# Fifteen rounds of two bits in place of thirty of one: the threshold search of a router on one Trainium2 core

## What is computed

```python
N, k = 4096, 1024                      # tokens; places of one expert
scores = jax.nn.softmax(xt @ Wr, axis=-1)      # (N, 8)
G, idx = jax.lax.top_k(scores.T, k)            # per expert: the k best tokens
X_in = xt[idx]
...
out = zeros.at[idx.reshape(-1)].add(contrib)
```

## Time and profile before

| | us |
|---|---|
| runs timed | 1288.48, 1290.49, 1291.82; median 1290.49 |
| profiled execution, span | 1295.1 |
| first count of the search to the copy of the threshold, in it | 637.92 to 684.86 |

### The profile page before, as it was taken

The page is one execution under the profiler, slowest core; times in us unless marked ns, Lnnn a source line. Parts: engine busy times, 40 slices in busy tenths (PEclk is TensorE's granted clock), DMA queues, the critical chain, the costliest instruction groups (busy, mean ns, idle before and its releaser), DMA issues. The chain is left out here.

```text
span 1295.1 us, 25137 instructions
## 1 busy us (share of the span) xinstructions
PE 975.8 (75%) x8604; PEld 662.5 (51%) x8604; DVE 805.3 (62%) x1683; ACT 639.2 (49%) x2132; POOL 430.4 (33%) x332
## 2 busy tenths in 40 slices
PE   6779998989899999985613769747348787867665
PEld 3456565656656565664503556534225454545454
DVE  5777758687777767564657514112136878559995
ACT  3565767767676767671101323112038777643322
POOL 2334333333342423321000857886611312200221
PEclk9789899999999998987555789888759999868967
DMA  6564343434443434431402123445310000000000
GB/s 198 150 182 107 92 123 88 119 96 113 102 113 100 113 83 107 104 91 42 102 0 62 45 59 69 61 73 129 31 66 1 1 2 1 1 1 9 17 17 25
DMA packets 89009, 93.62 MB, mean 72 GB/s; under 512 B 18800, under 2 KB 62304, under 8 KB 88944
## 3 DMA queue, kind: packets, MB, share of 16 engines
q1 hardware_dynamic: 78576, 84.12, 24.7%
q0 software_dynamic: 10368, 8.66, 4.7%
HBM read 24.36 MB, written 10.70 MB: 27 GB/s over the span
## 5 line engine op out<-in xcount | busy, mean ns | idle before, releaser
L835 POOL TENSOR_TENSOR qk_cos<-qk_raw,const 128x512 f32<-128x512 f32 x128 | 183.2, 1432 | 313.0 <-ACT qk_raw L589 313.0
L575 ACT ACTIVATE prob<-psS,neg_max 128x96 f32<-128x96 f32 x512 | 167.9, 342 | 86.5 <-DVE neg_max L670 85.7
L442 PE MATMUL psQ<-a_xnT,weights 128*128 128x512 f32 x250 | 146.0, 668 | 2.1 <-ACT a_xnT L621 1.4
L550 PEld LDWEIGHTS psO<-probT,v_windows 96*64 96x64 f32 x2048 | 73.7, 143 | 142.6 <-ACT probT L649 121.1
L550 PE MATMUL psO<-probT,v_windows 96*64 96x64 f32 x2048 | 91.8, 235 | 43.9 <-ACT probT L649 43.9
L685 DVE TENSOR_TENSOR qk_roped<-qk_cos,qk_swapped 128x512 f32<-128x512 f32 x128 | 119.0, 929 | 5.9 <-DVE qk_swapped L676 5.5
L1508 POOL DMA_INDIRECT sums<-ex_y,ex_index x64 | 97.6, 1525 | 39.5 <-issue 23.5
L1497 POOL DMA_INDIRECT ex_rows<-rows,ex_index x64 | 67.1, 1048 | 121.8 <-DMA ex_index<-lists 102.6
L575 ACT ACTIVATION_READ_ACCUMULATOR prob<-psS,neg_max 128x1 f32 x512 | 105.4, 206 | 0.0
L1442 ACT ACTIVATE ex_hidden<-ex_psH,ex_b 128x512 f32<-128x512 f32 x64 | 43.7, 687 | 114.4 <-PE ex_psH L1401 59.7
L649 ACT COPY probT<-psT 96x512 f32<-96x512 f32 x128 | 76.8, 600 | 46.5 <-PE psT L530 46.5
(11 more groups left out here) (317 smaller groups left out, 1936.2 us busy)
## 6 DMA issues: line engine op xcount, KB each, us to landing
qk_swapped<-qk_raw SPq DMA_DIRECT2D x512, 64.0 KB, 2.0
v_windows<-v_tok SPq DMA_DIRECT2D x32, 384.0 KB, 4.4
v_windows<-v_tok SPq DMA_DIRECT2D x32, 256.0 KB, 3.6
mod<-mod_rows SPq DMA_DIRECT2D x12, 512.0 KB, 6.0
ex_w<-in_L_ffn_W SPq DMA_DIRECT2D x16, 256.0 KB
v_windows<-v_tok SPq DMA_DIRECT2D x32, 96.0 KB, 2.1
rows<-rt_h SPq DMA_DIRECT2D x8, 256.0 KB, 2.4
sums<-rt_zeros SPq DMA_DIRECT2D x8, 256.0 KB, 2.7
```

Source lines behind the costliest of these rows:

```text
L442: last = nc.tensor.matmul(bank, k.wqkvT[:, col:col + P], xnT[:, :], start=True, stop=True)
L550: ins = nc.tensor.matmul(psO[D * j:D * j + D, i * P + a * HALF:i * P + (a + 1) * HALF], vw[:, par, a, t, hd], probT[:, 2 * j + i, a * HALF ...
L575: last = nc.scalar.activation(prob[:, s, 2 * j + i, :], psS[:, s, j, i * KW:(i + 1) * KW], ACT.Exp, bias=nmax[:, s, 2 * j + i:2 * j + i + ...
L835: nc.gpsimd.tensor_tensor(rcos[:, half, :], raw[:, half, :], k.const[:, K_COS:K_COS + T], ALU.mult).then_inc(cos_done, 1)
```

## The change

Each round settles two bits. There are three candidates a round, the settled bits with 1, 2 and 3 in the two present bits. VectorE counts three times, into three columns of `reached`; one matmul adds three columns. `met` compares the three totals with 1024 and sums how many candidates hold (0 to 3) into `passed`; `step` is that number times the weight of the lower present bit, as an integer; one operation ORs it with the settled bits and, in four columns, with 0 to 3 in the next two bits. Column 0 of `cand` is what is settled, and two buffers of `cand` take turns. The fifteen rounds are written out on both engines, so that all addresses and wait values are constants. The table of constants gets 4 x 16 columns in place of 31.

```diff
-LOOK = 5
+ROUNDS = BITS // 2
...
-K_END = K_BITS + BITS + 1
+K_END = K_BITS + 4 * (ROUNDS + 1)
...
-    t[:, K_BITS:K_BITS + BITS] = 2.0 ** np.arange(BITS - 1, -1, -1)
+    for r in range(ROUNDS):
+        t[:, K_BITS + 4 * r:K_BITS + 4 * r + 4] = np.arange(4) * 4.0 ** (ROUNDS - 1 - r)
...
-        sT, hitT = sb("rt_scoresT", [P, 2 * P]), sb("rt_hitT", [P, 2 * P], BF16)
-        same, bits = sb("rt_same", [P, P], BF16), sb("rt_bits", [P, BITS + 1], I32)
-        cand, drop, reached = sb("rt_cand", [P, 1], I32), sb("rt_drop", [P, 1], I32), sb("rt_reached", [P, 1], BF16)
+        sT, hitT = sb("rt_scoresT", [P, 2 * P]), sb("rt_hitT", [P, 3, 2 * P], BF16)
+        same, bits = sb("rt_same", [P, P], BF16), sb("rt_bits", [P, 4 * (ROUNDS + 1)], I32)
+        cand, met, passed, step = sb("rt_cand", [P, 2, 4], I32), sb("rt_met", [P, 3]), sb("rt_passed", [P, 1]), sb("rt_step", [P, 1], I32)
+        reached = sb("rt_reached", [P, 3], BF16)
...
-            with pe.Fori(0, BITS // LOOK) as turn:
-                for i in range(LOOK):
-                    pe.wait_ge(counted, turn * LOOK + i + 1)
-                    nc.tensor.matmul(psC[:, 0:1], same[:, :], reached[:, :], start=True, stop=True).then_inc(totals, 1)
+            for n in range(ROUNDS):
+                pe.wait_ge(counted, 3 * n + 3)
+                nc.tensor.matmul(psC[:, 0:3], same[:, :], reached[:, :], start=True, stop=True).then_inc(totals, 1)
...
-            own.mark(nc.vector.tensor_copy(cand[:, :], k.const[:, K_BITS:K_BITS + 1]))
+            own.mark(nc.vector.tensor_copy(cand[:, 0, :], k.const[:, K_BITS:K_BITS + 4]))
...
-            def look(turn, i):
-
-                n = turn * LOOK + i
+            def look(n):
+
+                now, then = cand[:, n % 2, :], cand[:, 1 - n % 2, :]
                 with nc.allow_low_precision("counts up to 256 are exact"):
-                    nc.vector.tensor_scalar(hitT[:, :], sT[:, :], cand[:, :].bitcast(F32), 0.0, ALU.is_ge, ALU.add,
-                                            accum_out=reached[:, :]).then_inc(counted, 1)
+                    for c in range(3):
+                        nc.vector.tensor_scalar(hitT[:, c, :], sT[:, :], now[:, c + 1:c + 2].bitcast(F32), 0.0, ALU.is_ge, ALU.add,
+                                                accum_out=reached[:, c:c + 1]).then_inc(counted, 1)
                 dve.wait_ge(totals, n + 1)
-                at = lambda table, n: table[:, bass.ds(n, 1)]
                 dve.wait_ge(search.sem, search.mark(nc.vector.tensor_scalar(
-                    drop[:, :], psC[:, 0:1], float(CAP), at(k.const, n + K_BITS), ALU.is_lt, ALU.mult)))
+                    met[:, :], psC[:, 0:3], float(CAP), 0.0, ALU.is_ge, ALU.add, accum_out=passed[:, :])))
+                dve.wait_ge(search.sem, search.mark(nc.vector.tensor_tensor(
+                    step[:, :], passed[:, :], k.const[:, K_BITS + 4 * n + 1:K_BITS + 4 * n + 2], ALU.mult)))
                 dve.wait_ge(search.sem, search.mark(nc.vector.scalar_tensor_tensor(
-                    out=cand[:, :], in0=drop[:, :], scalar=at(bits, n + 1), in1=cand[:, :],
-                    op0=ALU.bitwise_xor, op1=ALU.bitwise_xor)))
-
-            with dve.Fori(0, BITS // LOOK) as turn:
-                search.turn(turn)
-                for i in range(LOOK):
-                    look(turn, i)
-                assert search.n == search.per
+                    out=then, in0=bits[:, 4 * n + 4:4 * n + 8], scalar=step[:, :], in1=now[:, 0:1].to_broadcast([P, 4]),
+                    op0=ALU.bitwise_or, op1=ALU.bitwise_or)))
+
+            search.turn(0)
+            for n in range(ROUNDS):
+                look(n)
```

More of the change, by code:

```diff
@@ L962, in phase_router @@
         pe_turned, thr_ready = sem("rt_pe_turned"), sem("rt_thr_ready")
-        search = Tally(sem("rt_search"), 2 * LOOK)
+        search = Tally(sem("rt_search"))
         block = ctx.enter_context(nc.Block())
@@ L1119, in look @@
                 dve.wait_ge(search.sem, search.mark(nc.vector.scalar_tensor_tensor(
-                    out=cand[:, :], in0=drop[:, :], scalar=at(bits, n + 1), in1=cand[:, :],
-                    op0=ALU.bitwise_xor, op1=ALU.bitwise_xor)))
-            with dve.Fori(0, BITS // LOOK) as turn:
-                search.turn(turn)
-                for i in range(LOOK):
-                    look(turn, i)
-                assert search.n == search.per
-            nc.vector.tensor_copy(wide_thr[:, :], cand[0:E0, :].bitcast(F32).to_broadcast([E0, P])).then_inc(thr_ready, 1)
+                    out=then, in0=bits[:, 4 * n + 4:4 * n + 8], scalar=step[:, :], in1=now[:, 0:1].to_broadcast([P, 4]),
@@ L1130, in _ @@
+                    op0=ALU.bitwise_or, op1=ALU.bitwise_or)))
+            search.turn(0)
+            for n in range(ROUNDS):
+                look(n)
+            nc.vector.tensor_copy(wide_thr[:, :], cand[0:E0, ROUNDS % 2, 0:1].bitcast(F32).to_broadcast([E0, P])).then_inc(thr_ready, 1)
             dve.wait_ge(pe_turned, 3)
```

## The result

The changed kernel takes 1270.51 us (median of four runs, 1270.12 to 1273.03) where the kernel before takes 1290.16 in the same measurement (four runs, 1288.48 to 1291.82). The quotient of these two medians is 0.9848, or 19.6 us; the comparison on record, whose working isn't given, puts the ratio at 0.9875 with a 95% interval of 0.9849 to 0.9901: faster, by 16 us (13 to 19). I had forecast 1280.9 with a range of 1277.5 to 1286.0. The direction was right; the gain was undersized, and the median lies outside the range.

The account below looks back on a forecast made before the run. The search was taken as one VectorE-TensorE chain with nothing beside it, so time saved there leaves the kernel. Fifteen rounds of 2.50 us (37.5) against 46.9, plus 0.2 at entry, save 9.6: 1290.5 to 1280.9 us, range 1277.5 to 1286.0.

Parts of the forecast that it names:

- Three counts in a row: VectorE's three counts in each search round: 0.50 us from count to count, ends 0.41 and 0.57.
- met to step: In each search round, from the test of three totals to the weighting operation: 0.27 us, ends 0.19 and 0.36.
- TensorE to met: In each search round, from the matmul to the test of its totals: 0.23 us with fixed addresses, instead of 0.35.
- step to cand: In each search round, from the weighting operation to the one writing the next candidates: 0.20 us, upper end 0.35.
- cand to count: In each search round, from writing the candidates to the next count: 0.25 us, as in the kernel before.
- last count to TensorE: In each search round, from the third count to the matmul: 0.55 us, as in the kernel before.
- gap at the entry: From the score copy's end to the first count: 0.03 us without a loop instead of 0.25, 0.2 us saved.
- case E: More saved in the search: count to count 0.41 us and met to step 0.19, giving 1277.0 us; chance 0.02.
- A: Search gaps of 0.35 us stay despite fixed addresses: 4.1 us less saved, 1285.0 us; chance 0.12.
- B: Counts in a search round do not overlap, 0.57 us apart: 2.1 us less saved, 1283.0 us; chance 0.10.
- C: Written-out search code reaches VectorE late once or twice, 2.0 us or more each: 1282.9 or 1284.9 us; chance 0.05.
- D: Expert stage loses TensorE's higher clock after an emptier search: slower, 1293.5 us or 1296.5; chance 0.03.

Follow-up runs that it names:

- the delay put back: The changed kernel with 30 linked VectorE operations (13.8 us) between the search and the threshold copy: ratio to the kernel before 1.0010.
- counts_apart: The changed kernel with each round's second and third counts waiting on a semaphore for the one before: ratio to the kernel before 0.9905, search 37.7 us.
- no_step: The changed kernel with the step operation taken out of the chain in the first eleven rounds: search 31.1 us, ratio to the kernel before 0.9885.
- one_bit_written_out: The kernel before with its thirty one-bit rounds written out instead of looped, nothing else changed: search 38.9 us, ratio to the kernel before 0.9923.
- two_bits_in_loop: Two bits a round as in the changed kernel, but three rounds written out and twelve in a hardware loop: search 37.9 us, ratio to the kernel before 0.9913.
- after: The changed kernel in its first measurement: 1270.51 us, ratio to the kernel before 0.9875, search 33.9 us.
- after_again: The changed kernel measured once more, with more rounds: ratio to the kernel before 0.9892, search 33.9 us.
- three_bits: The changed kernel with three bits a round, seven counts in each of ten written-out rounds: search 38.8 us, ratio to the kernel before 0.9949.
- wide_table: The kernel before with its constants' table 33 columns wider, so nearly all later tensors lie 132 bytes further on: ratio to the kernel before 1.0003.
- after_beside: The changed kernel measured a third time, on the same chip as the variant without the step operation: ratio to the kernel before 0.9900.
- before: The kernel without the change, one bit a round in a loop: 1290.16 us median, search 47.6 us in its trace.

## Why the prediction was wrong, and where it was right

**What bounds it: right.** The time taken out of the search came out of the kernel, shown by the delay put back (1.0010, 0.9991 to 1.0030).

**Three counts in a row: the term that failed.** I took 0.50 us from count to count, between ends of 0.41 and 0.57. It is 0.40: the read costs no time of its own, since the next count starts together with it. The 0.09 that I added for the read came from ScalarE's row, another engine, and the 0.08 between small operations seemed to bear it out. 15 x 2 x 0.10 = 3.0 us of the miss. The Trainium skill's DRAIN rule (VectorE: DVE Perf Modes, "The DRAIN you can't avoid") would have given 0.57, still further off. The same section sends the reader on with "A next op that is not held starts earlier", which is what the trace shows; and where it says of eight copies in a row that the semaphore between them costs nothing extra, counts_apart shows 0.13 us for one between counts.

**met to step: too high.** 0.27 forecast, 0.21 measured, 15 x 0.06 = 0.9 us. I scaled down 0.55, a count's distance to TensorE, where to a linked VectorE operation it is 0.53 (counts_apart). And met lasts 0.16 us, though by my scaling a count over three columns should last 0.21. What the scaling most likely carried along is the scalar that a count reads from a tile. The earlier trace rows had the answer: an operation of that size with an immediate lasts 0.17, 0.22 with a scalar from a tile. In no_step cand loses the same 0.06.

**The other links: right to 0.01 us.** TensorE to met 0.22 (0.23 forecast), step to cand 0.20 (0.20), cand to count 0.26 (0.25), last count to TensorE 0.55 (0.55). The gap at the entry is 0.04 (0.03 forecast). Their reason, the addresses, held in one_bit_written_out and two_bits_in_loop.

**The sum.** 37.5 us forecast, 33.4 measured from first count to threshold copy; 3.0 + 0.9 and roundings are the 4.1 between them. With the right terms the forecast is 1290.5 - 13.7 = 1276.8 us, still 0.7 below my range: both open terms went to their favourable ends, or close to them, at once. I had priced exactly that as case E, at 1277.0, and gave it 0.02, since I took the middle of my bounds for likely on both. A bound at which a thing costs nothing is not a far-fetched one on an engine whose rows already overlap.

**The rest of the 19.6 us: not the change.** The prediction had about 1.5 us of spread around each case. The runs of the unchanged kernel on the chips used here went from 1280.9 to 1294.9, apart from the two left out. My estimate from that range is that four runs against four could differ by 5 us with nothing behind it. The two further measurements, 13.9 and 12.9 us, lie close to the 13.7 us of the search, and above the 9.6 forecast.

**The rivals.** A fell (addresses), B fell (0.40, and 0.53 only when forced). C: VectorE waits in the search for nothing but TensorE's 15 totals (4.2 us), so the written-out code was in time. By the Trainium skill's page on code fetched ahead (Runtime: NRT & Kernel Launch, "Instruction fetch mechanics") that was to be expected, and this trace agrees. D did not decide the time: with the delay put back or without, the rest is 597 to 605 us. But what it describes is there in one trace. The first 5.00 us of the experts' first matrix products, in after and in after_again:

```profile
717.60:722.60 5.00, 4.98 (x11) 1.91 (x12) 0.00 (x0) 3.91 (x5) 3.77 (x5) 1.00 0.25 57
```

```profile
720.90:725.90 5.00, 4.96 (x6) 2.09 (x7) 0.01 (x1) 2.57 (x3) 3.78 (x5) 0.50 0.23 56
```

At 0.50 from the first product of this kind (L1402) to the first of the next (L1411) it is 10.8 us, at 1.00 8.5. The distance is 8.4 or 8.5 in eleven of the thirteen traces, all four with one bit a round among them, and 9.2 in three_bits; two traces out of nine can't tell whether a shorter search makes it likelier. E was the mechanism that came. The constants' transfer, 880.5 KB instead of 864.0, landed in 6.1 us instead of 6.8, and the tensors' places cost nothing (wide_table).

## What to carry to other kernels

In a chain of tiny operations, count links, not operations: each small VectorE operation that waits for the one before costs 0.20 to 0.26 us here, and an independent one put into a wait cost nothing (no_step). Before doing more work per round to save rounds, write the loop out: fixed addresses took 0.10 to 0.15 us off every operation that had one from a register, and with the loop's turns that was 8.7 of the 13.7 us (4.0 when it comes second). And before fitting a story to the difference of two traces, take a second trace of the kernel before and cut both at the same instructions.

## What the runs showed of the hardware

- An accumulator read on VectorE and an independent operation behind it start together (both at 637.84 us in after, both at 637.66 in no_step). It costs time only when the next operation waits for its count: 0.53 us instead of 0.40.
- Small VectorE operations with a scalar read from a tile take 0.22 us (drop, cand), those with an immediate 0.16 to 0.17 (met, rt_need, cand in no_step). No run changed that alone.
- TensorE's clock differs between executions of one program at the same place. At the end of attention 1, stretches of after and after_again, columns as in the earlier trace rows:

```profile
1113.50:1123.50 10.00, 3.48 (x42) 2.60 (x40) 7.04 (x18) 2.84 (x8) 0.00 (x0) 0.99 0.00 1
```

```profile
1118.00:1128.00 10.00, 7.76 (x56) 5.96 (x56) 4.77 (x12) 2.72 (x9) 0.00 (x0) 0.53 0.00 1
```

  At 0.99 (2.4 GHz) the time from VectorE's last maximum of attention 1 to its first product in ffn 1 is 26.3 us, at 0.53 (nearly all at 1.2 GHz) 29.5. Five of the thirteen traces have 26.2 to 26.4 us, with 0.84 to 1.00 granted in that stretch, and eight 29.4 or 29.5, with 0.50; there are traces with and without the change in both groups. The ranking matmuls at the head of the experts' stage show it too: from the start of chosen to ex_rank 2.9 us in the trace of after (1.00 granted), 4.4 in that of before (0.55), but 4.6 in after_beside (0.50), which is the changed kernel again. The spans of after and after_again differ by 9.0 us: 3.2 of them lie here, 2.3 at the experts' first products (above) and 2.1 ahead of the score copy, which starts anywhere from 633.5 to 640.3 us in the thirteen traces.
- The eight pauses of TensorE in one execution of before have no cause that a run here shows. They stay open.
